# Two sparse expert layers: deeper rings, and the second product's weights copied by VectorE

## The reference, cut to what is touched

```python
def _L2_xattn_ref(x, context, Wg, bg, W1, b1, W2, b2):      # here called E2; FFN = 512
    logits = jnp.einsum('bsd,de->bse', context, Wg) + bg
    scores_topk, idx_topk = jax.lax.top_k(logits, 2)
    weights = jax.nn.softmax(scores_topk, axis=-1)
    combine = jnp.sum(jax.nn.one_hot(idx_topk, 8) * weights[..., None], axis=-2)
    h = jax.nn.relu(jnp.einsum('bsd,edf->bsef', x, W1) + b1)
    y = jnp.einsum('bsef,efd->bsed', h, W2) + b2
    return jnp.einsum('bsed,bse->bsd', y, combine)

def _L2_ffn_ref(x, w_router, w_gate, w_up, w_down):         # here called E3; I = 352
    ...                                                     # router, best two, normalised
    gate = jax.nn.silu(jnp.einsum('th,eih->eti', xf, w_gate))
    up = jnp.einsum('th,eih->eti', xf, w_up)
    down = jnp.einsum('eti,ehi->eth', gate * up, w_down)
    return jnp.einsum('eth,te->th', down, combine)
```

## Time and profile before

| | |
|---|---|
| time, median of 3 runs | 961.72 us (960.16 to 966.69) |
| span of the profiled execution | 1010.8 us |
| E2, first fetch to last send | 488.60 to 619.62 us |
| E3, first fetch to last send | 668.98 to 800.66 us |
| instructions | 24129 |

### The profile page before, as it was taken

One profiled execution on the slowest core, in us unless ns is written; L12 is line 12 of the kernel. 1 busy time (PEld: TensorE's weight loads), 2 busy tenths in 40 slices (PEclk: granted clock), 3 DMA queues, 4 the chain that ended last, 5 costly groups with the idle time before them and its releaser, 6 DMA issues.

```text
span 1010.8 us, 24129 instructions
## 1 busy us (share of the span) xinstructions
PE 783.2 (77%) x8041; PEld 646.4 (64%) x8041; DVE 608.2 (60%) x1568; ACT 486.4 (48%) x984; POOL 372.9 (37%) x492
## 2 busy tenths in 40 slices
PE   6998899999999789996477775667677559969005
PEld 3766787888888679985476664667676526644005
DVE  3886747777777667767353224632222368867895
ACT  3886434555444344432154435334444357745753
POOL 5663421111111331111566653155556535550810
PEclk9999699999999979999699989579989769978557
DMA  6300000000000000033332213101111300000001
GB/s 187 96 0 1 1 1 3 2 3 0 0 0 3 1 11 19 21 102 103 95 100 88 64 41 105 42 19 43 40 37 45 85 23 3 0 1 1 0 0 42
DMA packets 49218, 36.06 MB, mean 36 GB/s; under 512 B 7665, under 2 KB 44978, under 8 KB 49138
## 3 DMA queue, kind: packets, MB, share of 16 engines
q1 hardware_dynamic: 43420, 24.45, 8.5%
q0 software_dynamic: 4992, 10.23, 3.6%
q10 hardware_dynamic: 726, 0.33, 0.1%
HBM read 26.73 MB, written 8.26 MB: 35 GB/s over the span
## 4 chain that ended last, share of the span: by engine, by line
PE 67%; DVE 9%; another core or an unknown queue 6%; issue 5%; ACT 5%; DMA 3%; DVEq 2%; POOL 2%; ACTq 1%; SPq 1%; POOLq 0%
PE psum L2118 9%; PE psum L1464 7%; PE psum L2143 4%; PE psum L1034 3%; PE psum L976 3%; PE psum L954 3%; PE psum L939 3%; PE psum L2442 2%; PE psum L1431 2%; PE psum L1432 2%; PE psum L1433 2%; PE psum L323 2%; PE psum L1016 2%; PE psum L663 2%
## 5 line engine op out<-in xcount | busy, mean ns | idle before, releaser
L2118 PE MATMUL psum<-E_XT,E_weights 128*128 128x128 f32 x780 | 114.3, 298 | 52.4 <-ACT E_XT L2198 27.7
L2118 PEld LDWEIGHTS psum<-E_XT,E_weights 128*128 128x128 f32 x780 | 103.0, 209 | 61.2 <-ACT E_XT L2198 30.8
L2266 POOL DMA_INDIRECT y_scratch<-E_y,route_place_of x78 | 78.8, 1010 | 83.2 <-DVE E_y L2321 37.8
L2258 POOL DMA_INDIRECT E_rows<-rows_scratch,route_token_of x78 | 76.4, 979 | 32.1 <-issue 25.5
L1723 DVE SCALAR_TENSOR_TENSOR X<-psum,E_gates,X 128x128 f32<-128x128 f32 x256 | 71.7, 344 | 26.5 <-PE psum L1464 26.4
L1464 PEld LDWEIGHTS psum<-E_w,E_h 128*128 128x128 f32 x512 | 69.4, 198 | 11.5 <-issue 3.5
L2221 ACT ACTIVATE E_h<-psum,cols 128x128 f32<-128x128 f32 x156 | 44.5, 368 | 66.4 <-issue 31.3
L1548 ACT ACTIVATE E_h<-psum,cols 128x512 f32<-128x512 f32 x64 | 43.8, 687 | 67.8 <-PE psum L1433 67.7
L1464 PE MATMUL psum<-E_w,E_h 128*128 128x128 f32 x512 | 70.4, 282 | 4.8 <-DVE X L1723 3.8
L2311 DVE TENSOR_TENSOR E_h<-E_sg,psum 128x384 f32<-128x384 f32 x39 | 21.6, 554 | 77.5 <-remote 26.8
L203 POOL TENSOR_TENSOR rstd<-vareps,nhalf 128x4 f32<-128x4 f32 x24 | 24.6, 1029 | 75.0 <-DVE vareps L197 74.9
(11 more groups left out here) (346 smaller groups left out, 2160.2 us busy)
## 6 DMA issues: line engine op xcount, KB each, us to landing
routed_back<-y_scratch SPq DMA_DIRECT2D x16, 256.0 KB, 4.9
E_first<-in_L_xattn_W SPq DMA_DIRECT2D x1, 2048.0 KB, 8.6
L1w<-in_L_xattn_W SPq DMA_DIRECT2D x8, 256.0 KB, 4.7
rows_scratch<-xn SPq DMA_DIRECT2D x8, 256.0 KB, 2.3
E_w<-in_L_ffn_routed_w SPq DMA_DIRECT2D x28, 64.0 KB, 1.9
E_raw<-in_L_ffn_w_down SPq DMA_DIRECT2D x8, 176.0 KB
E_rows<-rows_scratch,route_token_of POOLq DMA_INDIRECT x78
y_scratch<-E_y,route_place_of POOLq DMA_INDIRECT x78
```

What stands on the lines that cost most here:

```text
L2118: mm = pe.matmul(out[:, c * P:(c + 1) * P], WE[:, p, (k0 + c) * P:(k0 + c + 1) * P], XT[:, p, :], start=True, stop=True)
L2258: pool.indirect_dma_start(out=xg[:, i % 4, :], out_offset=None, in_=rows[:, :], in_offset=bass.IndirectOffsetOnAxis(ap=disp.token_of[:, i: ...
L2266: pool.indirect_dma_start(out=yrows[:, :], in_=y[:, i % 3, :], in_offset=None, out_offset=bass.IndirectOffsetOnAxis(ap=disp.place_of[:, i: ...
```

## The change

- Rings of four for `XT`, `WE`, `h` and `y` (`RING`), of eight for `xg` (`ROWS`). To find room, `h` lies in `m.xn`, and `WE` (E2) or the new `WL` (E3) in `m.XNT`, which are not in use then.
- PE turns two tiles ahead (`AHEAD`), and the second products follow three tiles behind the first (`BEHIND`).
- DVE copies the second weights of each tile's expert to a fixed place, `WL` (`last`): 128x512 in E2, 128x384 in E3 (there with a register load of its own, `own_last`). PE reads `WL` and loads no register.
- POOL fetches seven tiles first, then `fetch(i+7)`, `send(i)`.
- E3's weights are turned in two parts per three tiles, at two places in PE's round.

```diff
+RING, ROWS = 4, 8
+AHEAD, BEHIND = 2, 3
...
+        xg, XT, y = sb("rows", [P, ROWS, D]), sb("XT", [P, RING, TILE]), sb("y", [P, RING, D])
         if gated:
+            WE, sg = sb("weights", [P, RING, W1.shape[2]]), sb("sg", [P, 2, C, TILE])
+            WL = m.XNT[:, 0:RING * C * D].rearrange("p (r c d) -> p r c d", r=RING, d=D)
+        else:
+            WE, WL = m.XNT[:, :].rearrange("p (r f) -> p r f", r=RING), sb("last", [P, RING, C, D])
...
+    h = m.xn[:, 0:RING * C, :].rearrange("p (r c) s -> p r c s", c=C)
...
         def second(i):
-            p = i % 2
-            e = pe.value_load(disp.expert[0:1, i:i + 1], min_val=0, max_val=E - 1)
+            p = i % RING
             pe.wait_ge(*h_ready(i + 1))
+            pe.wait_ge(*last_ready(i + 1))
             if i >= 2:
                 pe.wait_ge(*y_out(i - 1))
             for c in range(C):
-                mm = pe.matmul(Y[p][:, 0:P], h[:, p, c, :],
-                               W2[:, bass.ds(e, 1), c, :].rearrange("p o d -> p (o d)"),
-                               start=c == 0, stop=c == C - 1)
+                mm = pe.matmul(Y[i % 2][:, 0:P], h[:, p, c, :],
+                               WL[:, p, c, :], start=c == 0, stop=c == C - 1)
...
-        turn(0)
-        for i in range(NTILE):
-            first(i)
-            if i + 1 < NTILE:
-                turn(i + 1)
-            if i >= 1:
-                second(i - 1)
...
+        for i in range(AHEAD):
+            turn(i)
+        for i in range(NTILE + BEHIND):
+            if i < NTILE:
+                first(i)
+            if i + AHEAD < NTILE:
+                turn(i + AHEAD)
...
+            if i >= BEHIND:
+                second(i - BEHIND)
...
-        for i in range(3):
+        for i in range(ROWS - 1):
             fetch(i)
-        for i in range(NTILE + 2):
-            if i + 3 < NTILE:
-                fetch(i + 3)
-            if i >= 2:
-                send(i - 2)
+        for i in range(NTILE):
+            if i + ROWS - 1 < NTILE:
+                fetch(i + ROWS - 1)
+            send(i)
...
+            dve.tensor_copy(WE[:, i % RING, :], W1[:, bass.ds(e, 1), :].rearrange("p o f -> p (o f)")).then_inc(w_ready.sem, 1)
+            last(i, e)
+
+        def last(i, e):
+            if i >= RING:
+                dve.wait_ge(*y_ps(i - RING + 1))
+            dve.tensor_copy(WL[:, i % RING, :, :].rearrange("p c d -> p (c d)"),
+                            W2[:, bass.ds(e, 1), :, :].rearrange("p o c d -> p (o c d)")).then_inc(last_ready.sem, 1)
+
+        def own_last(i):
+            e = dve.value_load(disp.expert[0:1, i:i + 1], min_val=0, max_val=E - 1)
+            last(i, e)
...
+        for i in range(NTILE + BEHIND):
+            if gated and i < NTILE:
                 hidden(i)
+                own_last(i)
+            if not gated and i + AHEAD < NTILE:
+                weights(i + AHEAD)
+                rows_turned(i + AHEAD)
+            if i >= BEHIND:
+                output(i - BEHIND)
             if "prepare" in spec and i >= 4:
                 spec["prepare"](dve, i - 4)
```

More of the change, by code:

```diff
@@ L2069, in dispatched_experts, with turned_at @@
     m.split_free, m.weights_here = [], []
-    def turned_at(n):
-        return n - 2 if turns and 0 <= n - 2 < 3 * turns.E else None
+    def turned_at(i, half):
+        q, rest = divmod(2 * i + half - 2, 3)
+        return q if turns and rest == 0 and 0 <= q < 3 * turns.E else None
     def sync(sp):
@@ L2083, in sync @@
                 turns.load(sp, e)
-        for k in range(3):
-            sp.wait_ge(*y_sent[k](16 * uses(3, k)))
+        for k in range(RING):
+            sp.wait_ge(*y_sent[k](16 * uses(RING, k)))
         for g in range(NG):
@@ L2128, in first @@
                     pe.wait_ge(*h_ready(i - 1))
-                products(m.banks[2 + p], p, 0)
-                products(m.banks[4 + p], p, C)
+                products(gate_banks[i % 2], p, 0)
+                products(up_banks[i % 2], p, C)
             else:
@@ L2226, in scalar @@
             act.wait_ge(*spec["weights_here"])
-            weights(0)
-            rows_turned(0)
+            for i in range(AHEAD):
+                weights(i)
+            for i in range(AHEAD):
+                rows_turned(i)
             for i in range(NTILE):
-                if i + 1 < NTILE:
-                    weights(i + 1)
+                if i + AHEAD < NTILE:
+                    weights(i + AHEAD)
                 silu(i)
-                if i + 1 < NTILE:
-                    rows_turned(i + 1)
+                if i + AHEAD < NTILE:
+                    rows_turned(i + AHEAD)
             disp.gate_exps(act)
@@ L2255, in fetch @@
         def fetch(i):
[L2256 to L2258 removed]
+            if i >= ROWS:
+                pool.wait_ge(*xT_ps(i - ROWS + 1))
+            pool.indirect_dma_start(out=xg[:, i % ROWS, :], out_offset=None, in_=rows[:, :],
                                     in_offset=bass.IndirectOffsetOnAxis(ap=disp.token_of[:, i:i + 1], axis=0)
[L2260 removed]
+                                    ).then_inc(x_here[i % ROWS].sem, 16)
         def send(i):
@@ L2328, in vector @@
             dve.wait_ge(*spec["weights_here"])
[L2329 to L2332, removed]
-                hidden(i)
[L2334 to L2338, removed]
+            for i in range(AHEAD):
+                weights(i)
+            for i in range(AHEAD):
+                rows_turned(i)
+        for i in range(NTILE + BEHIND):
+            if gated and i < NTILE:
+                hidden(i)
+                own_last(i)
+            if not gated and i + AHEAD < NTILE:
+                weights(i + AHEAD)
+                rows_turned(i + AHEAD)
+            if i >= BEHIND:
+                output(i - BEHIND)
             if "prepare" in spec and i >= 4:
                 spec["prepare"](dve, i - 4)
-        output(NTILE - 1)
         disp.gates(dve)
```

85 lines of the change are left out of this document (41 added, 44 removed).

## The result

The changed kernel takes 1011.16 us (median of 4 runs, 1007.43 to 1012.52) against 961.15 for the one before: 1.05 times as long, 95% interval 1.0469 to 1.0532. The forecast was 987, its range 973 to 1003: the direction was right, the time lies outside the range, and the loss of 50.0 us is twice the forecast's 26.

What follows compares the result with a forecast made beforehand. Without stalls POOL was taken to bound both layers at 2.58 us a tile, PE next. 961.7 + 0 (load) + 26 (E2's wait) + 1 (E3) - 1 (rings) = 987.7, say 987; forecast 973 to 1003, wider range 957 to 1003.

Steps and rivals of the forecast that it cites:

- Main reading: In E2 and E3, the stalls belong to the recorded execution; the timed runs already have POOL's pace, 2.58 us a tile.
- the stalls: Signals of PE arriving 2 to 3 us after its work in E2 and E3, 55.6 us in the recorded span.
- Deeper rings and POOL's order: POOL's fetch(i+7) ahead of send(i) never waits; the rings save -6.5 to 0 us, taken as -1.
- the outermost bound of the parts: The upper end of the summed parts for the timed runs, 1011 us (+33 +3.9 +12.5); the lower end was 971.
- the first loop: In E2, DVE's last(j) waits for PE's second(j-4), and PE's first(j) for the XT(j) behind last(j): 3.09 us a tile.
- The added wait in E2: DVE's copy waiting for PE's second products makes E2's rounds 3.09 us against POOL's 2.58: +26 us, bounds +15 to +33.
- Ahead of the first send: In E2, 19 more PE records precede the first send: 2.3 to 4.6 us later, taken as 2.3.
- The clock: PE in E2 would be busy about 2.4 of 3.2 us, as now, so its clock stays at 0.93.
- E3: No loop in this layer; only a later start, +0.7 to +3.9 us, taken as 1, then POOL's 2.58 a tile.
- DVE's copies against POOL: DVE's copies do not hold up POOL's sends: taken as 0; in E3 39 copies could cost 0 to 12.5 us.
- the rival: Port lock: each new DVE copy holds POOL up for its own length, E3 pays 12.5 us, total 1000; chance 0.03.
- The register load: PE's 78 loads of 302 ns run beside the products; removing them gains the timed runs 0 us, other end -55.6.

Runs made afterwards that it cites:

- before again: The kernel before the change, unchanged, recorded once more: 962.35 us, ratio 0.9996.
- nine ahead: The kernel before with eight slots for fetched rows in place of four and POOL's fetches nine tiles ahead of its sends in place of five: 959.77 us.
- rings only: The changed kernel without DVE's copies of the last weights; PE reads W2 at a register address again, with its load: 969.3 us.
- E3 only: Layer E2 as in the kernel before, layer E3 as in the changed kernel: 965.43 us.
- load back: The changed kernel with TensorE's register load put back ahead of each second product, the register unused: 1022.12 us.
- ten ahead: The changed kernel with POOL's fetches in E2 ten tiles ahead of its sends in place of seven: 986.29 us.
- One expert: The kernel before without TensorE's register load; every tile's second products read the weights of expert 0: 962.81 us.

## Why the prediction was wrong in size

- **Main reading: right, its reason not.** The timed runs had POOL's pace in both layers; recorded again, before has E2's last send at 594.48, where the forecast put POOL's pace at 591.8. But that the loads "bring on the stalls" did not show: five recordings with PE's loads (before again, nine ahead, rings only, E3 only, load back) have none. What made that one recording 50 us longer stays open. The 6.5 us put down to what lies around a span are 1.7 to 1.8; most of the rest is in the layers, whose sends took 94.4 and 92.7 us for 91.6. One reading was off: the first products 2.22 us apart stand between two stalls, since that of 718.62 comes behind a wait of 2.35. The Trainium skill, "NOTIFIC — the notification-queue block", section 7.1 "Overflow: three behaviours, one of which stalls the engine", says that the recorder can hold engines back; that one recording of a program was longer than its others agrees with it and does not prove it.
- **The failed step is "Deeper rings and POOL's order"**: "its rows' slot was read by `turn(i-1)`, several rounds back, so it never waits". Its own wait indeed never counts. But I checked only that wait, not what the fetch is queued behind: `send(i-1)`, which waits for DVE's output, which stands behind `last`. This is the second loop. I took -1; it measured +24.9 (1011.16 - 986.29), or 21.7 in E2 of the traces. That the outermost bound of the parts, 1011, meets the measured time is chance: it is made of +33 for the first loop, 3.9 for E3's start and 12.5 for copies.
- **"The added wait in E2": the loop right, the total in part luck.** With eight or ten tiles ahead this loop is alone, a tile takes 3.09 and 3.08 us, and the time is 987.51 and 986.29, which is the forecast. A round without a turned part took 3.00 (557.30 to 560.30) for 3.09, as the signal to DVE's copy took 0.13 (559.49 to 559.62) and not 0.24; with the turned parts and `prepare` it is the 3.08. But the layer was forecast at 129.6 us from first fetch to last send (618.2 - 488.6) and took 125.3: 20.1 more than before recorded again, not 26, and E3 took 4.4 more, not 1.
- **"Ahead of the first send": mis-sized.** I counted records of PE (+2.3) and not that `output(0)` stands behind `last(5)`: +6.5 against the earlier trace rows, +7.3 against before recorded again. With ten ahead the first send came 17.2 us behind the first fetch, where the forecast had 13.9, and the sends then took 108.1, where it had 115.7: the start was too cheap by 3.3, the rest too dear by 7.6.
- **The clock, "I leave it at 0.93": it did not stay there.** Windows of E2 after (columns as in the earlier trace rows):

```profile
493.00:510.00 17.00, 11.32 (x73) 10.47 (x73) 5.04 (x14) 6.84 (x23) 7.43 (x8) 0.73 0.30 83
511.00:622.00 111.00, 77.21 (x583) 67.12 (x581) 49.58 (x134) 44.76 (x145) 63.67 (x62) 1.00 0.23 64
622.00:641.00 19.00, 14.56 (x89) 12.66 (x90) 5.04 (x18) 5.36 (x17) 7.78 (x8) 0.82 0.12 29
```

  The last 19 us run at 0.82; ten ahead has 1.00 from 511 us to its last send. My estimate of what this is worth is at most 19 x 0.18 = 3.4 us of the 24.9.
- **E3: within its bounds, sized too low.** +1 forecast with bounds 0.7 to 3.9; +2.4 by the times of E3 only (0.2 to 4.6), 3.3 by its trace, 3.7 in the changed kernel's.
- **DVE's copies against POOL, 0: right in sum, its reason not.** E3's sends take 92.6 us with 39 copies of 128x384 (median 0.36), 92.7 without. But the send of 566.35, which I held against the rival, had started before its copy. One that starts inside a copy waits for it (E3 after):

```profile
708.65 0.36 DVE L2318 COPY XNT<-E_last 128x384 f32 x1 [0.20 <-PE psum L2149]
708.76 1.12 POOL L2277 DMA_INDIRECT y_scratch<-E_y,route_place_of  x1 [0.30 <-issue]
```

  It takes 1.12 for the usual 0.99 and ends 0.87 behind the copy. The send of 526.43 likewise ends 0.85 behind its DVE instruction, which is a TENSOR_TENSOR and no copy. A TENSOR_REDUCE of the same length does not hold a send up (E2 after):

```profile
524.11 1.34 DVE L2689 TENSOR_REDUCE qw_scale<-qw_raw 128x36 f32<-128x1152 f32 x1
524.46 0.98 POOL L2277 DMA_INDIRECT y_scratch<-E_y,route_place_of  x1 [0.60 <-DVE E_y L2343]
```

  So the rival's wait exists, but only for the rest of a copy, and few DMAs start inside one: all 78 in E3 together take 76.8 us on POOL, 76.3 without the copies. The Trainium skill, "SBUF — State Buffer", section "Who interferes with whom", has whichever comes first, GpSimd or a DVE copy that takes the port pair they share, keep that pair for its whole instruction while the other waits; the trace agrees where the copy comes first (0.87 behind its end). That it is the ports is not shown here.
- **The register load, 0: right for the kernel before** (962.81 without it), but not because the loads "run beside the products". In before recorded again PE stands idle ahead of its second products in E2 (PE's waits, 488 to 645 us):

```profile
PE psum L2143 <- issue: 5.8, 14, 0.6
```

  One expert, without the load, has no such wait. It cost nothing because POOL set the pace.

In one sum, from the spans of the second recording of before (958.5) and of after (1009.5): E2 41.8, E3 3.7, the first fetch of E2 3.3 later (486.8 to 492.6 in these recordings, with the same code ahead of it), the end 2.2: 51.0.

## What to carry to other kernels

On a queue that runs in order, as POOL's does here (the fetch of 566.75 behind the send of 565.47), an instruction also waits for the waits of all that stand ahead of it. For every added wait, follow each later instruction of that queue, DMA issues too, to its readers, until the path ends or returns to the start; a path that returns is a loop, and its time divided by the tiles it advances is a pace. Work is far enough ahead when that pace is under the bound's: here fetching one tile further ahead took away 24 us, and one tile less cost 138. Before reasoning from a profile, hold its span against the times of the runs; where they differ by more than the runs among themselves, record again.

## What the hardware showed that was not expected

- One recording of a program can be 52 us longer than another (1010.8 and 958.5), with signals of PE arriving 2 to 3 us late; the spans of 70 other executions of it on record all lie between 957.0 and 967.1.
- Of E2's rows, 2.59 us pass from the start of a fetch to the transposition that waits for it (566.75 to 569.34), 2.87 in the round before (559.41 to 562.28). In a loop this latency counts in full; with ten tiles ahead PE waits for rows only twice.
- An indirect DMA of POOL that starts inside some DVE instructions is held until these end. In the 14 profiles, from 488 to 650 us, 121 start inside a 128x512 copy (0.43 us), or a TENSOR_TENSOR or TENSOR_SCALAR of over 0.7 us, with more than 0.15 us of it left; 118 of them end 0.81 to 0.87 us behind it. Of 28 that start inside a TENSOR_REDUCE of 1.2 to 1.3 us, 27 take their usual 0.97 to 1.02.
